# An attention layer's empty-row flag as a factor of its outputs, a bare reciprocal, and a new order of work in the first group and at the end

## What is computed

```python
q = (text_hidden @ Wq)...; k = (vision_tokens @ Wk)...; v = (vision_tokens @ Wv)...
scores = jnp.einsum('bhtd,bhsd->bhts', q, k) / scale
scores = jnp.where(mask, scores, -jnp.inf)
attn = jax.nn.softmax(scores, axis=-1)
attn = jnp.nan_to_num(attn, nan=0.0)
out = jnp.einsum('bhts,bhsd->bhtd', attn, v)
return out @ Wo
```

## Time and profile before

| | us |
|---|---|
| median of 3 runs | 381.88 |
| the profiled execution, whole | 381.85 |
| its span in the profile | 380.1 |
| PE busy | 347.1 (91%) |
| DVE busy | 305.0 (80%) |
| POOL busy | 244.8 (64%) |
| ACT busy | 224.5 (59%) |
| mean granted clock of PE | 0.969 of full speed |

### The profile page before, as it was taken

One profiled execution on the slowest core, in us unless ns is written; L12 is line 12 of the kernel. 1 busy time (PEld: TensorE's weight loads), 2 busy tenths in 40 slices (PEclk: granted clock), 3 DMA queues, 4 the chain that ended last, 5 costly groups with the idle time before them and its releaser, 6 DMA issues.

```text
span 380.1 us, 6948 instructions
## 1 busy us (share of the span) xinstructions
PE 347.1 (91%) x2240; PEld 307.7 (81%) x2240; DVE 305.0 (80%) x500; ACT 224.5 (59%) x401; POOL 244.8 (64%) x151
## 2 busy tenths in 40 slices
PE   4886689999999999999999989996989999898996
PEld 1764478888898888898898978896978997687996
DVE  3497679999989989989989997635467756769997
ACT  2485477578668668668667577741035465246772
POOL 4819188698698598599569499293335743745550
PEclk9998789999999999999999999999599999989999
DMA  7506566885885895895785786771106011133640
GB/s 231 179 2 152 131 140 146 204 198 129 209 182 130 200 204 120 200 207 121 169 193 128 171 180 155 184 224 31 54 9 196 19 55 55 29 87 102 188 137 28
DMA packets 33332, 52.07 MB, mean 137 GB/s; under 512 B 5792, under 2 KB 23328, under 8 KB 33312
## 3 DMA queue, kind: packets, MB, share of 16 engines
q1 hardware_dynamic: 33168, 51.56, 54.8%
q10 hardware_dynamic: 144, 0.26, 0.3%
HBM read 20.08 MB, written 0.26 MB: 54 GB/s over the span
## 4 chain that ended last, share of the span: by engine, by line
PE 65%; DVE 18%; issue 8%; SPq 3%; DMA 2%; POOL 2%; ACT 1%; DVEq 1%; ACTq 0%
PE bank L538 10%; PE pair L538 9%; PE bank L539 9%; PE bank L540 9%; PE pair L540 9%; PE pair L539 9%; DVE probs L1311 3%; SPq L262 3%; DVE ctx_raw L1322 2%; DVE rden L1278 2%; PE bank L774 2%; PE pair L730 1%; DMA resid<-in_x_dram 1%; POOL ctxT_lo L410 1%; PE pair L766 1%
## 5 line engine op out<-in xcount | busy, mean ns | idle before, releaser
L410 POOL TENSOR_TENSOR pT<-pT,pT_hi 128x1024 fp32r<-128x1024 f32 x60 | 142.5, 2405 | 40.3 <-ACT pT_hi L1010 40.1
L1000 ACT ACTIVATE probs<-probs,lowest 128x2048 f32<-128x2048 f32 x32 | 64.3, 2010 | 43.4 <-DVE lowest L1311 43.4
L539 PE MATMUL bank<-pT,ctx_hi 128*128 128x256 f32 x240 | 68.5, 285 | 0.0
L538 PE MATMUL bank<-pT_hi,ctx_lo 128*128 128x256 f32 x240 | 68.2, 284 | 0.2 <-POOL pT L410 0.2
L1010 ACT ACTIVATE pT_hi<-pT 128x1024 fp32r<-128x1024 f32 x60 | 61.5, 1050 | 11.7 <-DMA pT<-blocks 7.8
L540 PE MATMUL bank<-pT_hi,ctx_hi 128*128 128x256 f32 x240 | 68.1, 284 | 0.0
L538 PE MATMUL pair<-ctxT_hi,qk_lo 128*128 128x512 f32 x128 | 52.7, 411 | 5.6 <-DVE qk_lo L1258 3.1
L539 PE MATMUL pair<-ctxT_lo,qk_hi 128*128 128x512 f32 x128 | 51.4, 401 | 0.0
L540 PE MATMUL pair<-ctxT_hi,qk_hi 128*128 128x512 f32 x128 | 51.3, 401 | 0.0
L1311 DVE CUSTOM_DVE_ANT_0 probs<-pair,mask_bias,lowest 128x1024 f32<-128x1024 f32 x32 | 41.0, 1282 | 12.3 <-PE pair L540 12.2
L538 PEld LDWEIGHTS bank<-pT_hi,ctx_lo 128*128 128x128 f32 x240 | 45.3, 189 | 1.0 <-POOL pT L410 0.4
(11 more groups left out here) (231 smaller groups left out, 862.4 us busy)
## 6 DMA issues: line engine op xcount, KB each, us to landing
pT<-blocks SPq DMA_DIRECT2D x128, 128.0 KB, 2.3
pT<-ctx_raw SPq DMA_DIRECT2D x112, 128.0 KB, 2.3
ctx_raw<-ffn_experts_gate_up_dram SPq DMA_DIRECT2D x16, 256.0 KB, 2.9
wq<-in_L_xattn_Wq_dram SPq DMA_DIRECT2D x8, 256.0 KB, 2.6
wo<-in_L_xattn_Wo_dram SPq DMA_DIRECT2D x8, 256.0 KB, 3.0
blocks<-in_L_attn_w_q_dram SPq DMA_DIRECT2D x4, 512.0 KB, 4.0
blocks<-in_L_attn_w_dense_dram SPq DMA_DIRECT2D x4, 512.0 KB, 4.2
ctx_raw<-_L_ffn_experts_down_dram SPq DMA_DIRECT2D x16, 128.0 KB, 2.5
```

Of the source, the lines that this page charges most:

```text
L410: pool.tensor_tensor(dst, src, hi.bitcast(F32), ALU.subtract).then_inc(ready, 1)
L538: pe.matmul(dst, w[1], x[0], start=start, stop=False)
L539: pe.matmul(dst, w[0], x[1], start=False, stop=False)
L1000: act.activation(probs[:, j], probs[:, j], ACT.Exp, bias=lowest[:, p, j, 1:2], scale=-1.0, accum_out=den[:, p, j:j + 1]).then_inc(exps, 1)
```

## The change

1. `scale_rows`, `dsum` and its fill on POOL go. The reciprocal of `den` is written to `rden` itself. The flag is a factor of oT now: the scale operand of the ACT copy and the scalar of the DVE instruction that makes the lo part.
2. The denominators of a unit are made right behind the `add_out` that last read their buffer, before `fold_rest` and before beat 5's `mask_pair`.
3. In each group PE makes q before wk's transpose, and ACT and DVE copy them in that order. `out_project` comes behind the beat's `attend`.
4. Group 0: DVE takes the context's chunks 6 and 7 before the two `turn`s; `q_project(1)` comes behind the scores of beat 5; ACT puts off the rounding of chunks 1 and 2. Group 1 waits for the context's lo part in beats 2 and 6, not before it begins.
5. The end: four `turn_final` come ahead of the output products, four behind, `y_project` comes between the `attend_final`s, and ACT in place of DVE rounds the self-attention's first weight.

The short description that comes with the change also says "no dummy products". The diff removes none: all calls of `keep_warm` stay.

```diff
-            pool.memset(dsum[:], 1.0).then_inc(consts, 1)
...
                 if fold_on and m == 1:
-                    wk_transpose(g + 1)
                     q_project(g + 1, 0)
                     q_project(g + 1, 1)
+                    wk_transpose(g + 1)
                 if out_on and m == 2:
                     y_project(2 * (g - 2) + 1, g - 2)
-                if out_on and m == 3:
-                    out_project(2 * (g - 2) + 1, g - 2)
...
-                if y_on and m == 7:
-                    out_project(2 * (g - 1), g - 1)
...
                 if y_on and m in (6, 7):
                     attend(2 * (g - 1) + 1, 1, m - 6)
+                if out_on and m == 3:
+                    out_project(2 * (g - 2) + 1, g - 2)
+                if y_on and m == 7:
+                    out_project(2 * (g - 1), g - 1)
@@ PE, group 0
-                if m == 4:
-                    wk_transpose(1)
+                if m == 5:
                     q_project(1, 0)
                     q_project(1, 1)
+                    wk_transpose(1)
...
-            pe.wait_ge(ctx_lo_ready, B)
             for m in range(BEATS):
+                if m == 2:
+                    pe.wait_ge(ctx_lo_ready, 1)
+                if m == 6:
+                    pe.wait_ge(ctx_lo_ready, B)
                 beat(1, m, True, False, True)
@@ PE, the end
-            turn_final(0)
-            turn_final(1)
+            for f in range(4):
+                turn_final(f)
+            attend(LAST - 2, 1, 1)
             out_project(LAST - 3, G - 2)
-            attend(LAST - 2, 1, 1)
+            attend(LAST - 2, 1, 2)
...
-            attend(LAST - 2, 1, 2)
+            for f in range(4, 8):
+                turn_final(f)
             attend(LAST - 2, 1, 3)
-            for f in range(2, 8):
-                turn_final(f)
+            for c in range(2):
+                attend_final(c)
             y_project(LAST - 2, G - 2)
-            for c in range(4):
+            for c in range(2, 4):
                 attend_final(c)
@@ ACT
+                if isinstance(n, int):
+                    act.wait_ge(some_key_ready, p + 1)
                 act.wait_ge(done, count)
-                act.activation(oT_hi[:], src, ACT.Copy).then_inc(oT_hi_ready, 1)
+                act.activation(oT_hi[:], src, ACT.Copy, scale=some_key[:, p]).then_inc(oT_hi_ready, 1)
@@ ACT, group 0
             ctx_chunk(4)
-            ctx_round(1)
             ctx_chunk(5)
-            ctx_round(2)
             exp_row(0, 0)
...
             exp_row(0, 1)
-            for c in range(3, B * NCH):
+            for c in range(1, B * NCH):
                 ctx_round(c)
+            q_copy(1)
             wkT_copy(1)
-            q_copy(1)
@@ ACT, the end
             p_round(G - 1, 0, 2)
-            oT_copy(LAST - 1, O_FINAL, final_av, 4)
             p_round(G - 1, 0, 3)
+            oT_copy(LAST - 1, O_FINAL, 1, final_av, 4)
+            act.wait_ge(ld_wq2, 16)
+            act.activation(wq2_hi, wq2, ACT.Copy).then_inc(wq2_hi_ready, 1)
             yT_copy(LAST - 1)
@@ DVE
             def denominators(u, p):
 
-                scale_rows(u, p, 2 * u)
-                dve.wait_ge(rden_step, 2 * u + 1)
                 dve.wait_ge(exps, 2 * u + 2)
-                dve.reciprocal(dsum[:, p], den[:, p]).then_inc(rden_step, 1)
+                after(dve, added, 2 * (u - 1))
+                dve.reciprocal(rden[:, p], den[:, p]).then_inc(rden_step, 1)
...
+                dve.scalar_tensor_tensor(oT_lo[:], src, some_key[:, p], oT_hi[:].bitcast(F32),
+                                         ALU.mult, ALU.subtract).then_inc(oT_ready, 1)
...
                     add_out(2 * (g - 2), 2 * (g - 2), 0)
+                denominators(2 * (g - 1), 0)
                 fold_rest(g, 1)
...
                 mask_pair(g, 1)
-                denominators(2 * (g - 1) + 1, 1)
-                if fold_on:
-                    wkT_rest(g + 1)
                 mask_pair(g, 2)
                 if fold_on:
                     q_rest(g + 1)
+                    wkT_rest(g + 1)
...
                     add_out(2 * (g - 2) + 1, 2 * (g - 2) + 1, 1)
+                denominators(2 * (g - 1) + 1, 1)
                 mask_pair(g, 5)
-                oT_rest(2 * (g - 1), O_BANK[0])
-                denominators(2 * g, 0)
+                oT_rest(2 * (g - 1), O_BANK[0], 0)
@@ DVE, group 0
             mask_pair(0, 3)
+            ctx_chunk(6)
+            ctx_chunk(7)
             dve.wait_ge(mask_ready, B * NCH)
             turn(0, 0)
             turn(0, 1)
-            ctx_chunk(6)
-            ctx_chunk(7)
             mask_pair(0, 4)
             mask_pair(0, 5)
             any_key(1)
-            denominators(0, 0)
+            q_rest(1)
             wkT_rest(1)
-            q_rest(1)
@@ DVE, the end
             norm_apply(0, 1)
-            dve.wait_ge(final_av, 4)
-            round_q(0)
             xnT_rest(0, 1, WQK_BANK)
```

More of the change, by code:

```diff
@@ L123, in perceiver_layer @@
         den = sb("den", [P, B, J])
-        dsum = sb("dsum", [P, B, J])
         rden = sb("rden", [P, B, J])
@@ L400, in _ @@
             pool.memset(ones[:], 1.0).then_inc(consts, 1)
-            pool.wait_ge(consts, 8)
+            pool.wait_ge(consts, 7)
             def power(b, n):
@@ L1020, in oT_unit @@
             def oT_unit(u, p):
-                oT_copy(u, O_BANK[p], av, 4 * (u + 1))
+                oT_copy(u, O_BANK[p], p, av, 4 * (u + 1))
             def group(g, wq_on, fold_on, out_on, last=False):
@@ L1030, in group @@
                 p_round(g - 1, 0, 2)
-                if fold_on:
-                    wkT_copy(g + 1)
                 exp_row(g, 0)
@@ L1035, in group @@
                     q_copy(g + 1)
+                    wkT_copy(g + 1)
                 p_round(g - 1, 0, 3)
@@ L1098, in _ @@
             exp_row(G - 1, 3)
[L1099 to L1103, removed]
+            for f in range(2, 8):
                 final_hi(f)
             p_round(G - 1, 0, 0)
+            oT_unit(LAST - 2, 1)
             p_round(G - 1, 0, 1)
@@ L1323, in turn, with oT_rest @@
                               probs[:, j].rearrange("p (k q t) -> p k q t", q=QD, t=LN)).then_inc(turned, 1)
-            def oT_rest(n, src):
-                rest_of(oT_lo, src, oT_hi, oT_hi_ready, n, oT_ready)
+            def oT_rest(n, src, p):
+                dve.wait_ge(oT_hi_ready, n + 1)
+                dve.scalar_tensor_tensor(oT_lo[:], src, some_key[:, p], oT_hi[:].bitcast(F32),
+                                         ALU.mult, ALU.subtract).then_inc(oT_ready, 1)
             def yT_rest(n):
@@ L1332, in add_out @@
                 b = 1 - p
-                dve.wait_ge(rden_step, 2 * (LAST + 2) if isinstance(u, int) and u == LAST else 2 * (u + 2) + 1)
+                dve.wait_ge(rden_step, u + 1)
                 dve.wait_ge(out_psum, n + 1)
@@ L1345, in group @@
                     add_out(2 * (g - 2), 2 * (g - 2), 0)
+                denominators(2 * (g - 1), 0)
                 fold_rest(g, 1)
                 if out_on:
-                    oT_rest(2 * (g - 2) + 1, O_BANK[1])
+                    oT_rest(2 * (g - 2) + 1, O_BANK[1], 1)
                 mask_pair(g, 1)
-                denominators(2 * (g - 1) + 1, 1)
-                if fold_on:
-                    wkT_rest(g + 1)
                 mask_pair(g, 2)
@@ L1436, in _ @@
             fold_rest(0, 0)
-            dve.wait_ge(consts, 8)
             dve.wait_ge(mask_ready, 2)
             mask_pair(0, 0)
-            fold_rest(0, 1)
             dve.wait_ge(mask_ready, 4)
@@ L1444, in _ @@
             any_key(0)
+            fold_rest(0, 1)
             ctx_chunk(4)
@@ L1471, in _ @@
             group(G - 1, False, True, last=True)
-            final_lo(0)
-            final_lo(1)
+            for f in range(2):
+                final_lo(f)
             add_out(LAST - 3, LAST - 3, 0)
-            denominators(LAST, 1)
-            for f in range(2, 5):
-                final_lo(f)
-            oT_rest(LAST - 2, O_BANK[1])
-            for f in range(5, 8):
-                final_lo(f)
-            yT_rest(LAST - 2)
-            scale_rows(LAST + 1, 0, 2 * (LAST + 1))
-            add_out(LAST - 2, LAST - 2, 1)
-            scale_rows(LAST + 2, 1, 2 * (LAST + 1) + 1)
-            oT_rest(LAST - 1, O_FINAL)
+            denominators(LAST - 1, 0)
+            for f in range(2, 8):
+                final_lo(f)
+            oT_rest(LAST - 2, O_BANK[1], 1)
+            yT_rest(LAST - 2)
+            add_out(LAST - 2, LAST - 2, 1)
+            denominators(LAST, 1)
+            oT_rest(LAST - 1, O_FINAL, 1)
             yT_rest(LAST - 1)
@@ L1491, in _ @@
             norm_apply(0, 1)
-            dve.wait_ge(final_av, 4)
-            round_q(0)
             xnT_rest(0, 1, WQK_BANK)
-            oT_rest(LAST, O_BANK[0])
+            oT_rest(LAST, O_BANK[0], 0)
             round_kv(0)
```

6 lines of the change are left out of this document (3 added, 3 removed).

## The result

The changed kernel takes 376.69 us (375.26 to 377.89, 4 runs), the kernel before 381.93 (381.21 to 382.71, 4 runs): ratio 0.986, 95% interval 0.982 to 0.990. The forecast was 373.3 (368.5 to 377.0). The profiled execution took 377.27 us with a span of 375.5, 4.6 less than the 380.1 before.

What follows compares the result with a forecast made beforehand. PE was taken to bound the loops and the order of work groups 0 and 1, with DVE setting PE's waits. The terms -3.9 - 2.8 - 1.3 - 0.5 = -8.5 us gave 373.3 us, range 368.5 to 377.0.

Steps and rivals of the forecast that it cites:

- part 2: Group 0's new order: mask_pair(0, 7) starts at 40.4, not 43.40; gain -3.9 us, bounds -2.9 and -5.4.
- I'm wrong if the period stays 27.9: Sign against the forecast: the loops' period was to fall from 27.9 to 27.2 to 27.4 us.
- Part 3: Loops, groups 1 to 6: new order covers PE's waits of 3.2 us, less 0.4: -2.8, bounds -0.8 and -3.9.
- Part 1: Flag moved to oT: removing 18 products shortens no PE work in the loops; cost 0.4 us, bounds 0 and 2.4.
- Part 4: Group 7: the product's stall goes and attend covers the remaining wait: -1.3 us, bounds -0.6 and -1.6.
- Part 5: The end: covered waits -1.3, split_q delaying norm_apply +0.3, lower PE clock +0.5; sum -0.5 us, bounds 0 and -5.
- DVE gets in first at the end: Rival at the end: DVE starts before POOL, xn 2 us earlier, 371.3; with PE's clock kept, 368. Chance 0.17.
- The moves and POOL become the bound: Rival in the loops: PE waits for pT in each group, only the lower bounds hold, 377.5 us. Chance 0.13.
- The reciprocal inherits the stall: Rival in 7 groups: the reciprocal alone waits up to one POOL instruction, 2.375 us; 384 at 1.7 us. Chance 0.03.
- two tensor inputs in SBUF: On DVE: such instructions stall until POOL's running instruction is over; the one-input reciprocal isn't stalled.

Runs made afterwards that it cites:

- the kernel with two reciprocals: Changed kernel with a second reciprocal into a spare tensor ahead of each of the 16 reciprocals: 376.6 us, ratio 0.983 to the kernel before.
- orders_no_flag: Kernel before with the new orders of group 0 and the loops, products kept, no flag on the output, old end: 373.07 us, ratio 0.976.
- loops_only: Kernel before with only the loops' new order (q ahead of wk's transpose, out_project behind an attend): 377.52 us, ratio 0.988.
- flag_only: Kernel before with the flag moved from the denominators to the oT copies and oT_rest, 18 products gone, old orders: 381.85 us, ratio 0.996.
- recip_behind: Changed kernel with each reciprocal of the loops behind oT_rest instead of ahead of it: 371.97 us, ratio 0.972 to the kernel before.
- split_first: Changed kernel with POOL's split_q for query block 0 ahead of its last power: 370.03 us, ratio 0.965 to the kernel before.
- yt_behind_mask3: Changed kernel with yT_rest behind mask_pair(g, 3) instead of ahead of it: 376.28 us, ratio 0.983 to the kernel before.
- flag_one_input: Kernel before with its 128 x 2 product written as a tensor times a scalar by partition, one tensor input: 382.84 us, ratio 1.000.
- best_of: Changed kernel with split_q ahead of the last power, loop reciprocals behind oT_rest, yT_rest behind mask_pair(g, 3) and mask_pair(g, 7): 372.91 us, ratio 0.975.

## Why the forecast was right in direction and too large

**Range and sign** were right, the range by little and with luck. The sum was -8.5; the medians differ by 5.2, the profiled executions by 4.6. 376.69 lies 0.3 us inside the range. Groups 0 and 1 gave 1.0 us more than part 2 said (0.4 counted by stage); without that it would have been 377.1 to 377.7, outside. And one of the text's own signs came true, "I'm wrong if the period stays 27.9": it is 27.95.

**Part 2, groups 0 and 1: right.** -3.9 forecast, -4.87 measured, inside its bounds, and PE kept its clock this time (1.00 for 0.82). With the new order the clock isn't what gained: in the kernel with two reciprocals, the same up to there but for one instruction, it was 0.72 from 32.3 to 36.8, `mask_pair(0, 7)` came at 39.28 for 38.41, and `mask_pair(2, 0)` at 69.97 for 70.33. The forecast's 40.4 was too late by more than 1 us even at the lower clock. The order is enough: orders_no_flag keeps the products and gains 5.50, and the eight kernels with the new order and the flag start `mask_pair(2, 0)` between 69.47 and 70.85. What the text did not see is that the flag alone gains nearly as much (-4.44, with a kept clock), so that the two edits overlap: 2.53 and 4.44 alone, 4.87 together.

**Part 3, the loops' order: right by itself.** 3.2 us gross forecast for groups 1 to 6; loops_only gains 0.59 up to `mask_pair(2, 0)` and 3.04 in groups 2 to 6 (136.45 for 139.49), 3.63 together, and 0.77 in group 7.

**Part 1, the flag: the step that failed.** It said that DVE's and PE's ways to `y_project` "are about equal in length, so I take 0.4 us over all groups (bounds 0 and 7 x 0.34 = 2.4)". The runs show 3.7 us in groups 2 to 6 alone (140.15 for loops_only's 136.45), above the upper bound, and +3.25 with the old order (flag_only's 142.74 for 139.49). Against orders_no_flag (136.19), which differs from the changed kernel only by the flag and the end, it is 4.0. So it is shown that the flag's edit ate the gain. Two things were wrong. The reciprocal was priced by its own length, 0.17; with the wait for `add_out` it takes 0.36 and 0.23 of DVE's time, so with `oT_rest`'s 2 x 0.06 the price is 0.7 us a group. And it was taken as mostly hidden where it is paid in full: PE waits 0.70 us a group, and the period is 0.80 above that of loops_only. That recip_behind takes most of this away by order alone shows that the place is what costs; how it divides between the reciprocal and the rest is this sum and not an experiment. No wait of ACT for the flag shows in the trace. The oT copies with the scale take 0.45 to 0.48 us for 0.36 to 0.41, as forecast. The Trainium skill, ScalarE: Activation LUTs, What ACT_TABLE_LOAD costs, gives about 93 ns for a pointer operand; the trace agrees (the shortest are 0.450 for 0.357 us, the medians 0.456 for 0.378).

**Part 4, group 7:** -0.46 for -1.3, below the bounds. Not POOL's stream but ACT and DVE's order came next: `yT_rest` waits 2.24 us for ACT's yT copy, with `mask_pair(7, 3)` behind it. Moving it gives 0.84 of the 0.84 that was missing.

```profile
218.16 0.42 DVE L1267 TENSOR_TENSOR yT_lo<-bank,yT_hi 128x256 fp32r<-128x256 f32 x1 [2.24 <-ACT yT_hi L1024]
218.50 1.28 DVE L1304 CUSTOM_DVE_ANT_0 probs<-pair,mask_bias,lowest 128x1024 f32<-128x1024 f32 x1
```

**Part 5, the end:** the mechanism and nearly the size. From `mask_pair(7, 7)` to the first query product 26.52 us for 27.20, -0.7 (-1.0 forecast: -1.3 and +0.3); from there on it takes 0.75 more (117.04 for 116.29), where 0.5 was forecast for the lower clock. That size is uncertain: the six kernels with the old end take 115.50 to 116.67 there, the four with this end 116.20 to 117.32.

**Rivals.** "DVE gets in first at the end" happened in none of the four kernels with this end: POOL began 0.07 us ahead each time and `norm_apply` took 2.42. But split_first is its case by another way: 2.0 us as priced, and the clock 4.8 where the text had 3 to 4. "The moves and POOL become the bound" gave 377.5, near the time measured, but by another mechanism: recip_behind, with the same moves and the same POOL work in 27.33 us a group, rules it out. "The reciprocal inherits the stall": all 16 take 160 to 170 ns, no.

## What to carry to other kernels

Price a small instruction by the start-to-start gap it opens between its neighbours, its wait for the one just ahead included: here 0.17 us of work cost 0.36. Put what another engine waits for ahead of what nobody waits for: `oT_rest` ahead of the reciprocal and of one `mask_pair` gave back 0.62 us a group. A stalled instruction whose successor would wait anyway costs nothing, as in the loops here, so removing it there buys nothing. Where DVE and POOL start from one signal, see which of them could have run earlier: moving `split_q` by one place was worth more than the whole change.

## What the runs showed of the hardware

**Which DVE instructions wait for POOL.** The forecast said two tensor inputs in SBUF. The tensor times a scalar by partition, f32 and SBUF to SBUF, waits just the same (1046 ns at the median for 1064), and so does `norm_apply`, the same operation (2.42 us); the reciprocal never did in any kernel. The Trainium skill, SBUF — State Buffer, Who interferes with whom, names copy, cast and tensor_scalar as operations that can take both port pairs by a faster mode; for tensor_scalar the trace agrees. The other case, POOL behind a DVE instruction that began first, was not tested.

**PE's clock behind a break** isn't a matter of the break's length alone. In group 0 PE idles for 2.34 to 2.47 us ahead of a beat's scores (at 32.2 to 33.8) in all fourteen kernels. In four executions its clock was 1.00 from 32.3 to 36.8 (the changed kernel, yt_behind_mask3, flag_only, flag_one_input), in the other ten 0.62 to 0.77; the changed kernel and the one with two reciprocals have the same 2.34 us and 1.00 against 0.72. At the end, the 1.89 us of split_first and of best_of were followed by 1.00 and 0.57. What else decides is open. split_first's six runs lie between 369.13 and 370.20, those of best_of between 371.48 and 374.31.
